# Gathers into six buffers instead of three in three stages, and no memset between the gathers in two

## The reference

```python
h = relu(layernorm(x)); x = x + L0(h)   # typed attention over the edges
h = relu(layernorm(x)); x = x + L1(h)   # cosine gate and differences
h = relu(layernorm(x)); x = x + L2(h)   # sum over the neighbours, MLP 64-128-64
h = relu(layernorm(x)); x = x + L3(h)   # 4-head attention, second layernorm

# L1, the layer of the stages difference and propagate
h_src, h_dst = h[src], h[dst]
scale = norm(h_src) * norm(h_dst) + 1e-6
gate = exp(clip(relu((h_src * h_dst / scale) @ proj).sum(-1), -5, 5))
src_diff = segment_sum(h_src - h_dst, dst)
h_diff = segment_sum(src_diff[src] * gate, dst)
out = relu(h_diff @ W_ffn.T + b_ffn)

# L2, the layer of the stage mlp
agg = segment_sum(x[src], dst)
out = relu((x + agg) @ W0 + b0) @ W1 + b1
```

## Time and profile before

| | before |
|---|---|
| timed runs, median of 3 | 5672.16 us (5667.63 to 5672.7) |
| profiled execution, first to last instruction | 6105.6 us |
| PE busy in it | 4432.3 us (73%) |
| DVE busy | 4412.9 us (72%) |
| ACT busy | 2446.8 us (40%) |
| POOL busy | 3619.2 us (59%) |
| mean granted TensorE clock | 0.784 of full speed |

### The profile page before, as it was taken

How to read it: one execution, slowest core, us unless ns; L and a number is a source line. 1 busy time by engine, 2 the same in 40 slices (tenths; PEclk the granted TensorE clock), 3 DMA queues, 4 the chain that set the end, 5 groups by cost and what they waited for, 6 DMA issues and landing times. The chain is left out here.

```text
span 6105.6 us, 72124 instructions
## 1 busy us (share of the span) xinstructions
PE 4432.3 (73%) x17616; PEld 2513.0 (41%) x17681; DVE 4412.9 (72%) x7837; ACT 2446.8 (40%) x7859; POOL 3619.2 (59%) x3943
## 2 busy tenths in 40 slices
PE   0577776679999986999655546555787878777776
PEld 0455554534444434666444432222333334344443
DVE  5678787768888878999766656555666766666665
ACT  0567776624434432555433322211222333333333
POOL 1556655466666640000267668776777667777776
PEclk9888898889999998999755555555778866767776
DMA  9233234433434337999533324444555522222221
GB/s 360 100 103 105 100 117 131 131 76 84 88 82 88 86 71 200 285 286 287 165 87 86 85 75 108 105 103 99 135 144 143 140 76 65 66 65 61 64 63 37
DMA packets 833422, 725.15 MB, mean 119 GB/s; under 512 B 535904, under 2 KB 543010, under 8 KB 832880
## 3 DMA queue, kind: packets, MB, share of 16 engines
q1 hardware_dynamic: 534000, 513.27, 28.9%
q0 software_dynamic: 101440, 90.01, 8.3%
q10 hardware_dynamic: 197568, 117.25, 6.2%
HBM read 450.28 MB, written 273.76 MB: 119 GB/s over the span
## 5 line engine op out<-in xcount | busy, mean ns | idle before, releaser
L1382 POOL DMA_INDIRECT df_hs<-u,keep_idx x392 | 419.1, 1069 | 879.5 <-POOLq L243 701.9
L802 POOL DMA_INDIRECT t<-keep_ptr_pay,keep_scat_ptr x392 | 410.0, 1046 | 390.6 <-DVE den_df L659 138.3
L896 POOL DMA_INDIRECT sc_xg<-t,keep_gather x392 | 435.8, 1112 | 329.3 <-DVE sc_h L196 175.2
L1382 POOL DMA_INDIRECT hd_gat<-u,keep_idx x392 | 475.5, 1213 | 158.8 <-issue 116.5
L1909 POOL DMA_INDIRECT out_x<-hd_x,keep_scat_out x392 | 453.3, 1156 | 143.3 <-issue 118.5
L1382 POOL DMA_INDIRECT ml_gat<-u,keep_idx x392 | 399.8, 1020 | 158.9 <-issue 93.5
L1382 POOL DMA_INDIRECT pr_gat<-sd,keep_idxsd x392 | 408.6, 1042 | 137.1 <-issue 69.9
L1543 PE MATMUL df_ps_p<-keep_weights,df_prod 64*128 64x64 f32 x784 | 189.8, 421 | 271.7 <-ACT df_junk_p L1526 156.4
L1065 PE MATMUL sc_ps_r<-sc_qx,keep_weights 128*64 128x512 f32 x784 | 359.4, 601 | 31.3 <-DVE sc_prod L977 28.1
L1371 PE MATMUL at_ps_m<-at_vx,keep_msg_twice 128*128 128x512 f32 x784 | 361.7, 605 | 22.6 <-DVE at_vx L1262 22.6
L2049 PE MATMUL hd_ps_h<-keep_weights,hd_xb 128*128 128x128 f32 x784 | 245.7, 413 | 145.3 <-DVE hd_wn L1992 119.9
(11 more groups left out here) (313 smaller groups left out, 12478.9 us busy)
## 6 DMA issues: line engine op xcount, KB each, us to landing
u<-den_dh SPq DMA_DIRECT2D x196, 256.0 KB
t<-tab_row ACTq DMA_DIRECT2D x98, 272.0 KB, 11.3
tab_x<-in_x SPq DMA_DIRECT2D x98, 256.0 KB
den_dx<-in_x SPq DMA_DIRECT2D x98, 256.0 KB
out_x<-den_dx SPq DMA_DIRECT2D x98, 256.0 KB
sc_et<-in_etype_row SPq DMA_DIRECT2D x98, 256.0 KB
at_v<-vt SPq DMA_DIRECT2D x196, 128.0 KB
at_et<-in_etype_row SPq DMA_DIRECT2D x98, 256.0 KB
```

Source lines behind the costliest of these rows:

```text
L802: pool.indirect_dma_start(pairs, bass.IndirectOffsetOnAxis(ap=e.scat_ptr[:, c:c + 1], axis=0), e.ptr_pay[:, c, :], None, bounds_check=NP * ...
L896: pool.indirect_dma_start(xg[i][:, u, :], None, e.T0, bass.IndirectOffsetOnAxis(ap=e.gather0[:, b.n, u:u + 1], axis=0), bounds_check=NP - ...
L1382: pool.indirect_dma_start(gat[i][:, u, :], None, table, bass.IndirectOffsetOnAxis(ap=idx_all[:, c:c + 1], axis=0), bounds_check=rows - 1, ...
```

## The change

The gathered buffers of difference (`hs`), propagate and mlp (`gat`), and their semaphores, come in AHEAD = 6 copies instead of three. `Step.ring(6)` gives a group's copy and round among six. POOL waits for the consumer of the group six before, and the consumers read copy n mod 6. The memsets of `rest` in propagate and mlp, their tile and their semaphore are gone. All other buffers stay at three.

```diff
+AHEAD = 6
-REST = 128
+    def ring(self, size):
+        return Step(self.n, self.n // size, self.n % size, size)

-def gather(pool, table, idx_all, gat, gathered, st, pos, rows, rest=None, rested=None):
+def gather(pool, table, idx_all, gat, gathered, st, pos, rows):
...
                                 bounds_check=rows - 1, oob_is_err=False).then_inc(gathered[i], 16)
-        if rest is not None:
-            wait(pool, rested, st.n * TU + u)
-            pool.memset(rest[:, :], 0.0).then_inc(rested, 1)

 # difference
-        hs = [s.sb(f"hs{i}", [P, TU, D]) for i in range(U)]
+        hs = [s.sb(f"hs{i}", [P, TU, D]) for i in range(AHEAD)]
...
-                    wait(pool, turned, st.n - (U - 1), e.pool_passed)
-                    wait(pool, sq1, st.n - (U - 1), e.pool_passed)
+                    wait(pool, turned, st.n - (AHEAD - 1), e.pool_passed)
+                    wait(pool, sq1, st.n - (AHEAD - 1), e.pool_passed)
                     gather(pool, e.U1, e.idx1, hs, gathered, st, pos(st), 2 * EP)
-                run_groups(pool, body, U, 0)
+                run_groups(pool, body, AHEAD, 0)
...
-                        a.wait_ge(gathered[st.s], 16 * TU * (st.k + 1))
+                        r = st.ring(AHEAD)
+                        a.wait_ge(gathered[r.s], 16 * TU * (r.k + 1))
...
 # propagate
-        rest = s.sb("rest", [P, REST])
-        rested = s.sem("rested")
-        gat = [s.sb(f"gat{i}", [P, TU, D]) for i in range(U)]
+        gat = [s.sb(f"gat{i}", [P, TU, D]) for i in range(AHEAD)]
...
-                    wait(pool, gm_done, st.n - (U - 1), e.pool_passed)
-                    gather(pool, e.SD, e.idxsd, gat, gathered, st, st.n, EP, rest, rested)
+                    wait(pool, gm_done, st.n - (AHEAD - 1), e.pool_passed)
+                    gather(pool, e.SD, e.idxsd, gat, gathered, st, st.n, EP)
...
 # mlp: as propagate, with t_ready and e.U2
```

More of the change, by code:

```diff
@@ L1411, in difference @@
         ps_n = s.ps("n", [P, 2])
-        gathered, hd_in, same_in, sd_out = [s.sems(n) for n in ("g", "hd", "sa", "so")]
+        gathered = s.sems("g", AHEAD)
+        hd_in, same_in, sd_out = [s.sems(n) for n in ("hd", "sa", "so")]
         turned, last_done, hb_done, prod_done, diff_done, sd_done = [
@@ L1507, in body @@
                     if st.on():
-                        a.wait_ge(gathered[st.s], 16 * TU * (st.k + 1))
+                        r = st.ring(AHEAD)
+                        a.wait_ge(gathered[r.s], 16 * TU * (r.k + 1))
                         wait(a, sq1, st.n)
-                        a.activation(junk_s[:, :, :], hs[st.s][:, :, :], ACT.Square,
+                        a.activation(junk_s[:, :, :], hs[r.s][:, :, :], ACT.Square,
                                      accum_out=nacc[:, 0, bass.ds(st.n, 1)]).then_inc(sq1, 1)
@@ L1552, in body @@
                         i = st.s
-                        wait(pe, gathered[i], 16 * TU * (st.k + 1), e.pe_passed)
+                        r = st.ring(AHEAD)
+                        wait(pe, gathered[r.s], 16 * TU * (r.k + 1), e.pe_passed)
                         wait(pe, sd_done, st.n - (U - 1), e.pe_passed)
                         for u in range(TU):
-                            m = pe.transpose(ps_t[i][:, u * P:(u + 1) * P], hs[i][:, u, :], e.C["ident"])
+                            m = pe.transpose(ps_t[i][:, u * P:(u + 1) * P], hs[r.s][:, u, :], e.C["ident"])
                         m.then_inc(turned, 1)
@@ L1581, in propagate @@
         nrm = s.norm("n", TU)
-        gathered, same_in, x1_in, x2_out, h2_out = [s.sems(n) for n in ("g", "sa", "x1", "x2", "h2")]
+        gathered = s.sems("g", AHEAD)
+        same_in, x1_in, x2_out, h2_out = [s.sems(n) for n in ("sa", "x1", "x2", "h2")]
         gm_done, turned, agg_done, f_ready, relu_done, x2_done, x_ready, h_done = [
@@ L1641, in body @@
                     if st.on():
-                        i = st.s
-                        v.wait_ge(gathered[i], 16 * TU * (st.k + 1))
+                        i, r = st.s, st.ring(AHEAD)
+                        v.wait_ge(gathered[r.s], 16 * TU * (r.k + 1))
                         wait(v, turned, st.n - (U - 1))
-                        v.tensor_tensor(gm[i][:, :, :], gat[i][:, :, :],
+                        v.tensor_tensor(gm[i][:, :, :], gat[r.s][:, :, :],
                                         e.gate[:, bass.ds(st.n * TU, TU)].unsqueeze(2).broadcast_to([P, TU, D]),
@@ L1719, in mlp @@
         nrm = s.norm("n", TU)
-        gathered, own_in, same_in, x2_in, h_out, xh_out = [s.sems(n) for n in ("g", "own", "sa", "x2", "ho", "xo")]
+        gathered = s.sems("g", AHEAD)
+        own_in, same_in, x2_in, h_out, xh_out = [s.sems(n) for n in ("own", "sa", "x2", "ho", "xo")]
         t_ready, o_ready, agg_done, hh_done, h1_ready, hid_done, h2_ready, x3_done = [
@@ L1728, in body @@
                 def body(st):
-                    wait(pool, t_ready, st.n - (U - 1), e.pool_passed)
-                    gather(pool, e.U2, e.idx2, gat, gathered, st, st.n, EP + NP, rest, rested)
-                run_groups(pool, body, U, 0)
+                    wait(pool, t_ready, st.n - (AHEAD - 1), e.pool_passed)
+                    gather(pool, e.U2, e.idx2, gat, gathered, st, st.n, EP + NP)
+                run_groups(pool, body, AHEAD, 0)
             @block.sync
@@ L1835, in body @@
                     if st.on():
-                        i = st.s
-                        wait(pe, gathered[i], 16 * TU * (st.k + 1), e.pe_passed)
+                        i, r = st.s, st.ring(AHEAD)
+                        wait(pe, gathered[r.s], 16 * TU * (r.k + 1), e.pe_passed)
                         wait(pe, agg_done, st.n - (U - 1), e.pe_passed)
                         for u in range(TU):
-                            m = pe.transpose(ps_t[i][:, u * P:(u + 1) * P], gat[i][:, u, :], e.C["ident"])
+                            m = pe.transpose(ps_t[i][:, u * P:(u + 1) * P], gat[r.s][:, u, :], e.C["ident"])
                         m.then_inc(t_ready, 1)
```

## The result

The changed kernel takes 5599.22 us, the median of four runs (5595.33 to 5600.9), against 5671.07 (5667.63 to 5672.7) for the kernel before: ratio 0.9875, 95% interval 0.9861 to 0.9889, 72 us less. A second set of runs gave 5598.93 against 5662.65, ratio 0.989 (0.9874 to 0.9907).

A forecast was written before the change was run, and what follows sets the result against it. The prediction took POOL's own work to bound difference, propagate and mlp in the timed run. Memsets -70 us, buffers 0 and traffic 0 gave 5672 - 70 = 5602 us, range 5535 to 5682 us.

The forecast's parts named there:

- POOL's own work is the pace of the timed run: Difference, propagate and mlp: POOL's own work of 5.34, 5.77 and 5.64 us a group sets the timed run's pace.
- The argument from the 433 us: Whole kernel: profiled 6105.6 us against 5672.16 timed; the 433 us must come mostly from late counts, 167 from three stages.
- third rival: Propagate and mlp: consumers are the bound, memset hidden; mlp alone 5635 us (chance 0.12), both 5672 us (0.13).
- The choice between the two: Timed run of difference, propagate and mlp: paced by POOL, as taken, or by the consumers, its opposite.
- The memsets, 70 us: Propagate and mlp: removing 784 memsets saves 0.09 us each, taken as 70 us, bounds 0 and 173.
- The second rival: Propagate and mlp: gathers without a pause get slow, deciding from a mean of 1.13 us; 5745 us, chance 0.12.
- Six buffers, 0: Difference, propagate and mlp: POOL paces the timed run and has no buffer waits to remove; 0, bounds 0 and 183 us.
- What the run-ahead may push aside, 0: Shared DMA engines: gathers issued up to three groups earlier don't hold up SP's and ACT's transfers; 0 us.
- PE next in mlp: Mlp after the change: PE at 5.15 us a group is late next, 0.13 us behind POOL, limiting further saving.
- Difference stays within 15 us of 610: Difference in the profile after: POOL's buffer waits are kept and the length stays within 15 us of 610.
- its own last sign: Difference, which loses no POOL work: the forecast is wrong if it shortens by more than 20 us.
- its 39 us for propagate: Propagate in the profiled execution: 39 us saved despite late counts, little in mlp, from 6105.6 to some 6060 us.

The follow-up runs named there:

- clean profile: The kernel before, unchanged, profiled again in the condition in which it takes 5663 to 5671 us; this profile spans 5663.6 us.
- rest512: The kernel before with the memset of 512 columns instead of 128: 5919.29 us, ratio 1.0451 to the kernel before.
- half: The changed kernel without the gathers of tiles 2 and 3 of each group in difference, propagate and mlp: 5248.28 us, ratio 0.9265.
- 6125 set: The one set of runs, on chip 2, in which the unchanged kernel before took 6124.8 us (median of 22) instead of 5663 to 5671.
- six_only_b: The kernel before with six buffers and the memsets kept, where before takes 5663 us: 5660.12 us, ratio 0.9996.
- no_memset_b: The changed kernel with three buffers again, memsets out, where before takes 5663 us: 5594.54 us, ratio 0.9883 to the kernel before.

## Why the prediction was right

*POOL's own work is the pace of the timed run.* Shown three ways: by the clean profile, in which POOL waits for no buffer longer than its usual gap while the consumers wait for gathers; by `rest512`, whose 256 us are the added memset time and nothing less; by `half`, though that halves the transfers too. The argument from the 433 us was right in its outcome: the clean profile, with the time of the timed runs, has no late count. It was only half complete. Of the 442 us between the two profiles of before, the three stages give 91, 46 and 74 us, 211 in all, where the prediction counted 57, 37 and 73; 234 us lie ahead of difference, where it did not look, and heads gives nothing, as it said. But I took the two numbers for one thing, once with a profile and once without, and they were of two kinds of runs. The profiled executions are not slower than the others: those with spans of 5663.6 and 5593.5 us are timed at 5665.39 and 5595.33 us, the medians at 5671.07 and 5599.22. In the 6125 set the third rival holds, and a prediction for it would have had to be "no gain". The choice between the two was the weakest step and the one that decided; what spoke for it was the time of the timed runs, not the profile.

*The memsets, 70 us.* Measured 72 in the result and 64 in the second set. By stage: 29.4 us in propagate and 36.8 in mlp, where 0.09 x 392 = 35 were forecast for each. Propagate gave less because its gathers took 1060 ns instead of 1043, 0.017 x 392 = 7 us; in mlp it is 4 ns. The second rival, which was said to decide from a mean of 1.13 us, would put this down to the missing pause. The other runs outside the 6125 set don't bear that out: the mean in propagate is 1046 ns with the memset and six buffers, 1048 with one column, 1060 to 1065 without a memset, and 1071 with 512 columns, the longest pause of all. The cause of these 17 ns is open. That 72 lies so near to 70 is in part luck: the two stages gave 66, and another 4.7 us lie between the first gather of heads and the end, which no step had and the change doesn't touch. That piece lasts 1199 to 1206 us in the nine profiles outside the 6125 set, so this is its spread from execution to execution.

*Six buffers, 0.* `six_only_b`: 3 us, interval across zero. The reason given, that a buffer is read 11 us before it is wanted again, holds in kind, but the 11 us left out the landing and the reading. In the clean profile a group's last gather in difference ends at 2870.90, its transposes run from 2872.50 to 2873.56, and the buffer is wanted at 2881.62, 8.1 us later. Even at the pace of after the shortest such time in mlp, in `no_memset_b` with its three buffers, is 3.9 us.

*What the run-ahead may push aside, 0.* The share of the DMA engines in mlp goes from 0.61 to 0.64, and of the loads only `same` is waited for in difference, once, 3.4 us after and 3.2 in the clean profile of before.

*PE next in mlp.* The step said 5.15 us a group for PE, 0.13 us behind POOL. That number is from a stretch with a mean granted clock of 0.78. In the clean profile of before it is 0.89, and PE's busy time 454 / 98 = 4.63 us a group; in `half` mlp took 456 us in all, 91 less than in the changed kernel. PE was never 0.13 us behind.

*Wrong on the profile.* "POOL's waits gone in propagate" and "1.30 us from gather to gather" came out. "Propagate shorter by 20 to 60 us" came out only against the clean profile, 29 us; against the earlier trace rows it is 632 to 561, 71 us. "Difference stays within 15 us of 610", and keeps POOL's waits, did not: it lasts 534 us without such waits, since the profile ahead of the prediction is of the other kind; between the clean profile and the one after it is 534 and 534. By its own last sign, difference shorter by more than 20 us, the forecast would have been called wrong; the sign compared two kinds of runs. And the forecast that the changed kernel's profiled execution would take 6060 us rested on the same mistake. Even among runs with late counts its 39 us for propagate were not there: without the memsets propagate lasts 646 us in the 6125 set, against 633 with them.

## What to carry to other kernels

Compare the span of the profile with the timed runs before pricing anything: 6105.6 against 5671 was no detail but another bound, and a profile taken again would have shown it. Then ask of each engine what its own work with its unavoidable gaps adds up to per group; here this sum, and not the busy share of 59%, named POOL. Then see that the consumers wait for it. More buffers remove waits for buffers and nothing else; where the waits of a clean profile are zero they are worth zero.

## What the runs showed of the hardware

- The same kernel on one core takes 5663 to 5671 us or about 6125 us, from one set of runs to the next, both with a granted clock of 0.50 or 0.51 (1.2 GHz) over difference. Where it takes over 6100, DVE starts a multiply of difference 1.8 us or more behind the recorded end of the transposes it waits for, 39 times in the profile ahead of the prediction and 36 to 41 times in each of the four profiles of the 6125 set. In the clean profile it starts 0.03 to 0.05 us behind that end, 97 times of 97, and none of the other profiles with all gathers at 5592 to 5927 us has a late one. The cause is open. The 6125 set is the only one on chip 2, and the others are on chips 9, 10 and 14: it may be that chip, or something that changes with time on any chip. No chip was used in two sets, so the record can't tell.
- In the earlier trace rows PE's products end at 3207.70 and their waiters start at 3213.93 and 3214.66, so the end in the row is not when the count came. The Trainium skill bears on it: "Perfetto Trace Analysis", section "Summary: the profiler window per engine type", calls TensorE's end an estimate. The rows agree so far that a late PE is found in the rows of its waiters; whether the products themselves took longer or only their count was late, no row tells.
- POOL stands 0.30 us between two indirect DMAs for which it has nothing to wait (119.1 us in 391 gaps of propagate after), and a memset can take up 0.13 us of it. A memset of float32 takes 117, 221 and 541 ns for 1, 128 and 512 columns.
- As POOL's pace in mlp rose, TensorE's mean granted clock there rose from 0.89 of 2.4 GHz in the clean profile to 0.91, and to 0.98 in `half`, over 3588 to 4020 us of its profile.
